# Two-layer sequence kernel: the next chunk's solved-system product moved behind the spread product, VectorE's spread ahead of the expert weighting, the head sums next to norm 2's variance

## What is computed

```python
x = layernorm(x + delta_attention(x))   # layer 0: delta rule, chunks of 32 tokens, 4 heads of 32
x = layernorm(x + experts(x))           # layer 0: 8 experts, each computed for all tokens, 2 gated in
x = layernorm(x + linear_scan(x))       # layer 1: gated linear recurrence
x = layernorm(x + gated_mlp(x))         # layer 1: 512 wide, two hidden layers

# delta rule, chunk i of every sequence and head; T solves the chunk's triangular system
u, w   = T @ v, T @ k_beta
attn_i = q_i @ k_i.T * causal
u_new  = u_i - w_i @ S
o_i    = q_i @ S + attn_i @ u_new
S      = S + k_i.T @ u_new

# experts
for e in range(8):
    out += gate[:, e] * (gelu(tokens @ w1[e].T) @ w2[e].T)
```

## Time and profile before

| | us |
|---|---|
| median of 3 runs | 971.48 (969.74 to 971.53) |
| the profiled execution, its own time | 968.62 |
| its span, first to last instruction | 966.8 |
| PE busy / DVE / ACT / POOL | 847.7 / 657.4 / 489.4 / 451.4 |
| mean granted clock of TensorE | 0.916 of full speed |
| one turn of the steady loop (spread product to spread product, 624.90 to 711.85) | 86.95 |

### The profile page before, as it was taken

One profiled execution on the slowest core, in us unless ns is written; L12 is line 12 of the kernel. 1 busy time (PEld: TensorE's weight loads), 2 busy tenths in 40 slices (PEclk: granted clock), 3 DMA queues, 4 the chain that ended last, 5 costly groups with the idle time before them and its releaser, 6 DMA issues.

```text
span 966.8 us, 12028 instructions
## 1 busy us (share of the span) xinstructions
PE 847.7 (88%) x3810; PEld 647.8 (67%) x3810; DVE 657.4 (68%) x1252; ACT 489.4 (51%) x757; POOL 451.4 (47%) x411
## 2 busy tenths in 40 slices
PE   5898689678885988998899899989999999999996
PEld 3676568466644776676678667866876787676664
DVE  2789947568825878687777658767775877677442
ACT  3473424632256245633664484457437544766743
POOL 0333488125410268599445435634453455256333
PEclk9897678757895699999999999999999999999998
DMA  3133230520020202000400110020003000000000
GB/s 120 34 106 112 77 109 26 160 77 1 0 77 0 62 17 77 1 1 0 110 1 1 41 47 0 0 65 22 0 0 87 0 0 0 12 1 1 11 12 11
DMA packets 37720, 35.72 MB, mean 37 GB/s; under 512 B 1584, under 2 KB 30512, under 8 KB 37680
## 3 DMA queue, kind: packets, MB, share of 16 engines
q1 hardware_dynamic: 37680, 35.22, 12.9%
HBM read 21.85 MB, written 13.37 MB: 36 GB/s over the span
## 4 chain that ended last, share of the span: by engine, by line
PE 45%; DVE 24%; ACT 12%; issue 10%; POOL 7%; DMA 1%; DVEq 0%; ACTq 0%; POOLq 0%; SPq 0%
PE bank L395 45%; DVE tpm L1198 2%; DVE tmp L1195 2%; DVE sexp L1331 2%; DVE spread L1315 2%; POOL fbl L1063 1%; DVE m L1470 1%; POOL acc L1071 1%; DVE yg L1341 1%; ACT L937 1%; POOL fbl L1097 1%; DVE a L1398 1%; DVE xtl L1135 1%; POOL tmp L1014 1%; POOL tpm L1017 1%
## 5 line engine op out<-in xcount | busy, mean ns | idle before, releaser
L1063 POOL TENSOR_TENSOR fbl<-hf,fbh 128x512 fp32r<-128x512 f32 x64 | 81.9, 1280 | 149.0 <-DVE fbh L1367 149.0
L832 ACT ACTIVATE hf<-bank 128x512 f32<-128x512 f32 x64 | 38.4, 599 | 195.8 <-PE bank L395 185.8
L395 PEld LDWEIGHTS bank<-pk,spread 128*128 128x128 f32 x640 | 89.3, 221 | 32.5 <-DVE spread L1315 19.6
L395 PE MATMUL bank<-pk,spread 128*128 128x64 f32 x640 | 92.3, 306 | 20.7 <-DVE spread L1315 15.6
L1097 POOL TENSOR_TENSOR fbl<-hf,fbh 128x512 fp32r<-128x512 f32 x32 | 43.3, 1353 | 99.0 <-DVE fbh L1429 99.0
L1071 POOL TENSOR_TENSOR acc<-acc,yg 128x512 f32<-128x512 f32 x48 | 68.0, 1416 | 39.3 <-DVE yg L1341 39.3
L1365 DVE TENSOR_TENSOR fbl<-hf,fbh 128x512 fp32r<-128x512 f32 x64 | 60.1, 939 | 33.1 <-ACT fbh L836 33.1
L395 PE MATMUL bank<-fbl,wmh 128*128 128x512 f32 x128 | 60.6, 473 | 9.4 <-DVE yg L1341 8.9
L395 PE MATMUL bank<-fal,wfh 128*128 128x512 f32 x160 | 65.8, 412 | 3.0 <-ACT hf L863 1.6
L1341 DVE TENSOR_TENSOR yg<-bank,gb 128x512 f32<-128x512 f32 x64 | 43.8, 685 | 33.3 <-PE bank L395 33.3
L1091 POOL TENSOR_TENSOR fal<-hf,fah 128x512 fp32r<-128x512 f32 x32 | 41.2, 1289 | 49.8 <-DVE fah L1424 49.8
(11 more groups left out here) (222 smaller groups left out, 2321.3 us busy)
## 6 DMA issues: line engine op xcount, KB each, us to landing
pack<-pk SPq DMA_DIRECT2D x7, 1280.0 KB, 6.8
pk<-pack SPq DMA_DIRECT2D x7, 1280.0 KB, 7.1
ws<-in_wf SPq DMA_DIRECT2D x11, 256.0 KB, 3.9
xs<-in_xh SPq DMA_DIRECT2D x8, 262.0 KB, 4.2
xt<-in_xh SPq DMA_DIRECT2D x8, 262.0 KB, 2.9
ws<-in_wm SPq DMA_DIRECT2D x8, 256.0 KB, 2.9
tt<-ttp SPq DMA_DIRECT2D x4, 512.0 KB, 2.7
out<-f SPq DMA_DIRECT2D x8, 256.0 KB, 3.0
```

The costliest lines, as they stand in the source:

```text
L395: return P.matmul(out, lhsT, rhs, start=start, stop=stop, skip_group_check=skip)
L832: A.activation(hf[:, 0, :], bank[4][:, :], ACT.Gelu).then_inc(S["gelu_done"], 1)
L1063: G.tensor_tensor(fbl[:, s, :], hf[:, 1, :], f32(fbh[:, s, :]), ALU.subtract)\
```

## The change

Four places are edited; no instruction is added or dropped.

1. PE: `delta_wu` of chunk n + 1 goes from the end of odd e to right behind `delta_attn` of chunk n, in e = 0, 2, 4.
2. POOL: `t_spread` of chunks 2 and 3, in e = 1 and 3, goes ahead of the sum acc.
3. DVE: `delta_spread` of the next chunk goes ahead of `gated` in odd e.
4. PE, `tails`: the head sums go from ahead of `glu(f, 2)` to behind it, next to norm 2's variance.

```diff
--- before.py
+++ after.py
@@ -568,6 +568,8 @@
                         output_product(f)
                     if a is not None:
                         (delta_state if e % 2 else delta_attn)(a, e // 2)
+                    if a is not None and e % 2 == 0 and e < E - 2:
+                        delta_wu(a, e // 2 + 1)
                     if a is not None and e == 4:
 
                         pe.wait_ge(S["x_in"], 16 * a + 16)
@@ -576,8 +578,6 @@
                         if f is not None and e == 1:
                             pe.wait_ge(*after("d4", f + 1))
                         down(m, e - 1)
-                    if a is not None and e % 2 and e < E - 1:
-                        delta_wu(a, e // 2 + 1)
                     if f is not None and e == E - 1:
                         if a is not None:
                             pe.wait_ge(*after("mix_act", a + 1))
@@ -636,12 +636,12 @@
                     pe.wait_ge(*after("gb_ready", E * last))
                     pe.wait_ge(*after("yg_ready", E * last))
                     glu(f, 1)
+                if f is not None:
+                    glu(f, 2)
                 if a is not None:
                     pe.wait_ge(S["osq_done"], a + 1)
                     pe.wait_ge(*after("o_copied", CN * a + CN))
                     mm(bank[2][:, :], head_w, a2[:, :]).then_inc(S["oss_done"], 1)
-                if f is not None:
-                    glu(f, 2)
                 if m is not None:
                     var_product("2", m, m2, 1)
                 if s1 is not None:
@@ -1062,6 +1062,9 @@
                         s = (e % 2) * HC + 1
                         G.tensor_tensor(fbl[:, s, :], hf[:, 1, :], f32(fbh[:, s, :]), ALU.subtract)\
                             .then_inc(S["lo1"], 1)
+                    if a is not None and e in (1, 3):
+                        t_spread(a, e // 2 + 2)
+                    if m is not None:
                         if e:
                             pool.wait_ge(*after("yg_ready", k))
                             if e == 1:
@@ -1070,8 +1073,6 @@
                                 pool.wait_ge(*after("acc_ready", (E - 1) * m + e - 1))
                             G.tensor_tensor(acc[:, :], (x1 if e == 1 else acc)[:, :], yg[:, (e - 1) % 2, :], ALU.add)\
                                 .then_inc(S["acc_ready"], 1)
-                    if a is not None and e in (1, 3):
-                        t_spread(a, e // 2 + 2)
                     if inv == 1 and e == 0:
                         solve_init(3)
                     if inv == 1 and e >= 4:
@@ -1382,10 +1383,10 @@
                             V.tensor_copy(x3h[:, :], x3[:, :]).then_inc(S["x3_hi"], 1)
                             dve.wait_ge(S["x3_hi"], 2 * x + 2)
                             tt(x3l[:, :], x3[:, :], f32(x3h[:, :]), ALU.subtract).then_inc(S["x3_ready"], 1)
+                    if a is not None and e % 2 and e < E - 1:
+                        delta_spread(a, e // 2 + 1)
                     if m is not None and e:
                         gated(m, e - 1)
-                    if a is not None and e % 2 and e < E - 1:
-                        delta_spread(a, e // 2 + 1)
                 if s1 is not None:
                     gram_rows(s1, 1)
                 if a is not None:
```

## The result

The changed kernel takes **987.9 us** (median of 4 runs, 986.1 to 988.7) against 971.3 (969.7 to 971.5): 1.0172 times the time before, interval 1.0154 to 1.019. The forecast was 975.3 and its range ended at 979.5: the sign was right, the size was not. In the profiled execution the time is 986.09, the span 984.3 us and the mean granted clock 0.911, where before it was 966.8 and 0.916; the other three executions have 0.906. In the table of experiments further down, medians and the split of the span are over all executions of a kernel, while the ratios leave out those more than 1.5% above the fastest one of their kernel (three of twelve for edit 4 alone, three of six for the kernel with two more gaps).

The account below looks back on a forecast made before the run. The prediction took the chain through DVE to bound the loop's expert pairs, by a hair. Its terms, 1.8 + 1.8 - 0.1 + 0.5 + 1.0 - 1.2 = +3.8 us, gave a median of 975.3, range 969.5 to 979.5.

Parts of the forecast that it names:

- The pair in the loop: Steady loop, each expert pair: chain loses 0.60 us, PE's stretch gains 0.80 uncovered, +0.20 a pair; four turns +1.8.
- Edit 2 "costs nothing in the loop": POOL's reordering in the loop: costs nothing, as POOL is busy for only 23.43 of 44.50 us.
- (a): Tile 0's delta stage: moved products delay PE, part comes back as the clock rises earlier; +1.8 us, ends +0.8 and +2.6.
- (b): Tile 0's experts: one product hides in a wait, spreads come 0.60 earlier, two products follow waits; -0.1 us.
- (c): Tile 1: chunk 1's product delays DVE by some 0.8, chunk 2's hides in a wait; +0.5 us, ends 0 and +1.7.
- (d): Tile 2: POOL's texp ends late, so PE waits 0.8 with everything behind it; +1.0 us, ends 0 and +2.
- Edit 4, −1.2: Six tail stages: the product that releases silu 3 comes 0.2 us earlier in each; -1.2 us, ends 0 and -2.4.
- The sum: Whole kernel: all terms of the loop, the stages ahead of it and the tails together, +3.8 us.
- rival 3: Much slower by the clock: longer waits bring 1.2 GHz stretches, about 981 us, steady dense stage's clock below 1.00; chance 0.07.
- Rival 1: Faster: waits for the spread were the cost and shrink by 0.60 each, about 966 us; chance 0.14.

Follow-up runs that it names:

- the kernel with two more gaps: Changed kernel, next chunk's product behind odd expert's state product, unread matmuls ahead of spread products, plus 22 around recurrence wait and 7 in first tail: 957.71 us (0.979).
- behind the state product: Changed kernel with the next chunk's solved-system product behind the odd expert's state product, ahead of down: 962.37 us, ratio 0.994 to the kernel before.

## Why the prediction was right or wrong

**The pair in the loop** was right in mechanism: chain less 0.60, PE stretch plus the product, no cover. The price of the product was mis-sized: "costs 0.80 us" is start to start with the next product of its old place; in the new one it is 0.87. The chain gave 0.58. So +0.30 a pair where +0.20 stood, 0.72 a tile where 0.45 stood, and the last turn's spreads agree.

**Edit 2 "costs nothing in the loop"** was read as worth nothing either, and that is false: with the three other edits in and this one left out, the kernel takes 26 us more. The prediction named who waits for the weighting on PE (down), and overlooked who waits on POOL: acc, and texp behind it. It keeps edit 1 from costing far more; the forecast's sum did not suffer, since edit 2 was in. Edit 2 by itself was not run.

**(a) Tile 0's delta stage, +1.8**: 2.6 to chunk 3's spread, and 5.8 to the next stage's first. The step that failed is "part comes back as the clock rises earlier": it rose at about 171 us, where before it had risen by 157, and all the products in between took twice their time. **(b) −0.1**: −0.14 (5.91 to 5.77), the right number by luck: a gain of 2.7 at chunk 1 and a loss of as much at chunk 2, where a new wait of 2.04 us stood ahead of chunk 1's spread product and the 10 us behind it ran at 0.56 and 0.75. **(c) Tile 1, +0.5**: +3.3 (7.73 to 11.04). The wait for chunk 2's spread grew from 1.15 to 1.45 us, and the clock fell behind it, where it had not before:

```profile
354.21 2.66 PE L395 MATMUL bank<-pk,spread 128*128 128x64 f32 x16 [1.45 <-DVE spread L1316]
...
355.00:362.00 7.00, 7.00 (x26) 5.58 (x26) 2.16 (x4) 0.45 (x1) 2.75 (x2) 0.53 0.00 0
```

**(d) Tile 2, +1.0**: −1.1 (13.06 to 11.94). The wait for texp did not come; POOL, which was to be late by 0.8, ended it at 451.81, and PE took it at 451.98 without idle time. The wait for chunk 2's spread fell from 1.46 to 0.54 us, and what followed ran at 1.00 (450 to 460), where before it had run at half clock from 439.66 on for some 3 us (0.74 over 440 to 445):

```profile
450.55 1.26 POOL L1048 TENSOR_TENSOR texp<-tb,cst 128x512 f32<-128x512 f32 x1
...
451.98 1.06 PE L395 MATMUL bank<-pk,texp 128*128 128x64 f32 x8
```

**Edit 4, −1.2**: 0.2 a tail, as worked out; in the runs' times it is lost in the scatter.

**The sum** was +3.8. The work grew by 5.6 us (892.7 against 887.2), so the path terms as a whole were not far off. The other 10.6 are the clock share. The step of the prediction that failed is thus the clock ahead of the loop: (a) let it rise earlier, and (b) to (d) put further time at 1.2 GHz at nothing. It was left to rival 3, at a chance of 0.07, with the wrong test: the steady dense stage kept its 1.00, and the clock fell ahead of the loop and in stretches of tails. The prediction held the loop's waits, which grow by 0.2 us, against it, and left out that PE stands at waits of 1 to 4 us in the four stages ahead of the loop, several of which grew (1.94 to 2.84, 1.92 to 2.50, 1.15 to 1.45, 0.76 to 1.30, and a new one of 2.04), while others shrank (4.34 to 4.21, 2.08 to 1.51, 1.46 to 0.54). It should have been priced there: half-clock work behind a wait of 1.94 was in the very rows read the earlier trace rows. The rule in the Trainium skill (TensorE: Matmul & The Clock Gate, HAM oscillation), that idle gaps throttle TensorE and what follows starts cold, agrees with the changed kernel with and without matmuls in its waits (clock share 90.6 against 83.1 us), and with the gap of 7.23 us. It does not tell when waits of 1 to 3 us are followed by a fall: one order had both, and with the wait filled the clock fell too. **Rival 1** (faster) was right about edits 2 to 4 (0.9896 times the time before), and wrong about edit 1.

What stays open: whether a given wait is followed by a fall differs from one execution to the next, and one profile a kernel doesn't tell the odds; and the loop's 6.6 us of clock share under edit 1 come from means of spans and clocks, not from one place in a trace; in the profiles more of the loop's cost is path.

## What to carry to other kernels

Work that is moved from beside a chain to ahead of it is paid in full, even on an engine that "waited" there; before moving it, look whether the new place is still beside the chain (here behind the state product: −0.6% instead of +1.7%), and whether the old one was not as good (the product unmoved, with the other edits: −1.0%, not told apart from −0.6%). Edits of a set are not independent: an order on one engine that makes a value late needs its partner on the next (1012.0 us without edit 2, 986.2 with it). And where PE waits ahead of work that it bounds, cost that work at the lower clock too, and split mean span into span times clock and the rest, over several executions, before explaining a difference from one trace.

## What the runs showed of the hardware

The clock's share (span less span times granted clock) is large, 64 to 104 us of the span in these kernels, and it varies in one kernel with a scatter of 4 us, more than the rest of the span has (1.3 us). In the changed kernel it was 0.51 over 20 us in which the profile shows PE busy throughout (150 to 170 us), behind one wait of 2.84; with the wait at 1.94, executions of one order gave 0.52, 0.85 and 1.00, and with the wait filled one gave 0.66. Behind the gap of 7.23 us the clock did not vary: the stretch of 20.2 us ran at 0.50 in every profile without matmuls in the gap, and took 14.7 us with them. Those twenty-two matmuls whose result nobody reads, in and behind one gap of 7.23 us, made the kernel 0.7% faster than the one without them (955.8 against 962.4, each beside its own runs of before: 0.9859 and 0.994). And a DVE cast took 1.49 us beside POOL's addition (621.76, above) and 0.41 while POOL was idle:

```profile
627.76 0.41 DVE L1368 CAST fbh<-hf 128x512 fp32r<-128x512 f32 x1
```
